# Attention slots with the products in another order, and three input projections of the second layer inside the last two slots

## The reference, cut to what matters

```python
# layer 0, for each sample b
x = normalise(x * s1)
q, k = heads(x @ Wq.T * q_dc), heads(x @ Wk.T * k_dc)
v_flat = x @ Wv.T * v_dc * s2
attn = softmax(q @ k.T * scale)                    # 16 heads of 256 x 256
out = (attn @ heads(v_flat)) @ Ww.T * w_dc + v_flat @ Wu.T * u_dc
x1 = x_in + out
# layer 1, for each sample b
xr, gate = split(x1 @ W_in.T)                      # 512 + 512 channels
xc = silu(causal_conv4(xr + t_emb) + b_conv)
xn = layernorm(xc); Bm, Cm, dt = split(xn @ W_xproj.T)
h = clip(h * ad + bd * xt, -10, 10) for each of 256 tokens; y = C h + D * xn
x2 = x1 + y * silu(gate) @ W_out.T
```

## Time and profile before

| | us |
|---|---|
| median of 3 runs | 580.69 (579.54 to 583.43) |
| the profiled execution, whole | 581.57 |
| its span in the profile | 579.8 |
| TensorE busy in the span | 481.0 (83%) |
| VectorE busy | 430.4 (74%) |
| ScalarE busy | 253.7 (44%) |
| slots 0 to 7 | about 57.8 to 265 |
| convolutions and tokens | to about 318 |
| scan over the tokens | about 368 to 579.8 |

### The profile page before, as it was taken

How to read it: one execution, slowest core, us unless ns; L and a number is a source line. 1 busy time by engine, 2 the same in 40 slices (tenths; PEclk the granted TensorE clock), 3 DMA queues, 4 the chain that set the end, 5 groups by cost and what they waited for, 6 DMA issues and landing times.

```text
span 579.8 us, 8410 instructions
## 1 busy us (share of the span) xinstructions
PE 481.0 (83%) x3000; PEld 283.4 (49%) x3000; DVE 430.4 (74%) x744; ACT 253.7 (44%) x504; POOL 194.2 (33%) x211
## 2 busy tenths in 40 slices
PE   1867888899898979879999860579999999999996
PEld 1753646567566645636999650113333333333333
DVE  2837254766756665863997995499999999999994
ACT  3331666667565645546787686024231111111111
POOL 6304303123030200000550295339876334434332
PEclk9966799999999989887999995599999999999999
DMA  8785375764846550101044447565654433443310
GB/s 343 300 154 109 56 145 112 146 118 88 152 102 137 95 115 2 37 2 36 1 175 144 133 141 184 166 222 188 200 174 91 153 107 107 124 128 111 99 31 24
DMA packets 44629, 71.80 MB, mean 124 GB/s; under 512 B 18825, under 2 KB 33545, under 8 KB 41468
## 3 DMA queue, kind: packets, MB, share of 16 engines
q1 hardware_dynamic: 40684, 67.55, 44.5%
q0 software_dynamic: 528, 3.55, 1.6%
q10 hardware_dynamic: 3376, 0.16, 0.3%
HBM read 41.88 MB, written 23.02 MB: 112 GB/s over the span
## 4 chain that ended last, share of the span: by engine, by line
PE 51%; DVE 24%; ACT 9%; DMA 6%; issue 3%; POOL 3%; SPq 2%; ACTq 0%; DVEq 0%; POOLq 0%
DVE win L1660 9%; ACT ex L682 6%; PE bank L980 6%; PE bank L1316 6%; PE bank L1276 5%; PE bank L1028 5%; PE bank L927 5%; PE bank L1287 5%; DVE z L1660 5%; PE bank L965 4%; PE bank L1007 3%; PE bank L950 3%; PE bank L998 3%; PE bank L1222 2%; DVE lnb_rep L1660 2%
## 5 line engine op out<-in xcount | busy, mean ns | idle before, releaser
L1482 DVE TENSOR_REDUCE mx<-bank 128x2 f32<-128x512 f32 x128 | 81.9, 686 | 80.2 <-PE bank L950 79.7
L1276 PE MATMUL bank<-xst,bst 128*128 128x512 bf16 x256 | 82.2, 390 | 41.2 <-DMA bst<-bd_d 24.9
L682 ACT ACTIVATE ex<-bank 128x512 f32<-128x512 f32 x128 | 69.8, 597 | 55.5 <-PE bank L965 55.3
L1660 DVE CUSTOM_DVE_ANT_0 win<-win,bank,hi 128x512 f32<-128x512 f32 x96 | 71.8, 748 | 3.4
L1276 PEld LDWEIGHTS bank<-xst,bst 128*128 128x128 bf16 x256 | 24.8, 98 | 94.8 <-DVE win L1660 31.0
L455 POOL TENSOR_TENSOR qk<-qk,part 128x512 f32<-128x512 f32 x16 | 19.7, 1233 | 138.2 <-ACT part L618 138.2
L950 PE MATMUL bank<-kst,qst 96*128 96x256 bf16 x256 | 49.8, 288 | 5.6 <-issue 3.4
L927 PE MATMUL bank<-xnT,w 128*128 128x256 f32 x192 | 50.5, 419 | 3.7 <-ACT xnT L603 3.6
L965 PE MATMUL bank<-qst,kst 97*128 97x256 bf16 x256 | 48.0, 283 | 4.0 <-ACT ex L682 1.9
L563 POOL TENSOR_TENSOR yg<-yT,gateT 128x128 f32<-128x128 f32 x60 | 29.4, 528 | 60.1 <-ACT yT L860 60.1
L980 PE MATMUL bank<-ex,vp 128*32 128x256 f32 x512 | 36.5, 405 | 12.9 <-ACT ex L682 12.9
(11 more groups left out here) (190 smaller groups left out, 917.0 us busy)
## 6 DMA issues: line engine op xcount, KB each, us to landing
qk_d<-part SPq DMA_DIRECT2D x64, 96.0 KB, 2.5
xs_d<-xpart SPq DMA_DIRECT2D x16, 384.0 KB, 4.6
xst<-xs_d SPq DMA_DIRECT2D x15, 384.0 KB
xn_d<-xc SPq DMA_DIRECT2D x16, 256.0 KB, 3.4
xtk<-xn_d SPq DMA_DIRECT2D x64, 64.0 KB
xst<-xs_d SPq DMA_DIRECT2D x15, 256.0 KB
bd_d<-zeros POOLq DMA_DIRECT2D x1, 3468.0 KB, 13.0
qst<-qk_d SPq DMA_DIRECT2D x8, 384.0 KB, 4.6
```

What stands on the lines that cost most here:

```text
L682: nc.scalar.activation(ex[:, n // 4, n % 4, :], bank[6 + n % 2][:, :], ACT.Exp, scale=SCALE)\
L1276: mm(bank[t % 4][:, :], bst[:, slot, t % RS, :], xst[slot][:, t % RS, :], start=True, stop=True)\
L1482: v.tensor_reduce(mx[:, :, STACKED[n]:STACKED[n] + 1], bank[4 + n % 2][:, :].rearrange("p (t k) -> p t k", t=HALVES), AX.X, ALU.max)\
L1660: v._custom_dve(bass.dve_ops.TENSOR_ADD_SAT, out=zst[t % ZR], in0=zst[(t - 1) % ZR], in1=bank[t % 4][:, :], s0=hi[:, t:t + 1], s1=0.0).the ...
```

## The change

In `sample(b)`, TensorE starts with `transpose_xn(b + 2)`, before `weigh(b - 1, 3)` and `turn_maxima(b)`; `v_tokens(b + 1)` moves from behind the maxima to behind heads 10 and 11; `weigh(b, 1)` moves behind heads 8 and 9, `weigh(b, 2)` behind heads 12 and 13, and `project_att` in front of heads 8 and 9. Heads 14 and 15 are done as pairs, maxima first. ScalarE's list follows: `take_xn` before `take_maxima`, `take_v` after the exponential of head 13, `take_weighed(b, 0)` after that of head 11.

In slot 6, `project_v(5)` and `project_v(6)` stand between the maxima and the scores, and `project_in(0)` is cut into halves of two channel blocks with heads between. In slot 7, `project_v(7)` and `project_in(1)` stand before the scores, and `project_in(2)` is made in two halves near the end. The first half of `project_in(3)` follows the slot, its second half follows `to_tokens(0)`. ScalarE copies the projections and does the last tap in single pieces of one channel block between exponentials (`projection_piece`, `tap_piece`). On VectorE `convolve(0)` moves from the end of slot 6 into slot 7, behind `attend(5)` and `add_skip(7)`; `attend(7)` moves behind `convolve(2)`, and `project_att(7)` behind `to_tokens(2)`. No operation is added or removed, only their order and the waits.

```diff
+            def projection_piece(b, c):
+                act.wait_ge(s["xr_done"], b * 2 + 1 + c // 2)
+                if b >= 2 and c == 0:
+                    act.wait_ge(s["conv_done"], b - 1)
+                ins = nc.scalar.activation(xrp[:, b % 2, c, TAPS - 1:],
+                                           bank[(4 if b else 2) + c // 2][:, (c % 2) * S:(c % 2 + 1) * S],
+                                           ACT.Identity, bias=cond[:, c, b:b + 1])
+                if c == CT - 1:
+                    ins.then_inc(s["xr_in"], 1)
...
             def sample(b):
                 project = b + 2 < B
-                take_maxima(b)
                 if project:
                     take_xn(b + 2, 2)
+                take_maxima(b)
                 if b >= 1:
                     take_weighed(b - 1, 1)
-                if b + 1 < B:
-                    take_v(b + 1)
                 if project:
                     take_qk(b + 2, 0, 2)
                     take_qk(b + 2, 1, 3)
+                if b == B - 2:
+                    act.wait_ge(s["ld_l1"], 16 * 11)
+                    act.wait_ge(s["const_pool"], 2)
+                elif b == B - 1:
+                    last_tap(0)
                 exponentials(b, 0, 2)
                 if project:
                     second_cast(b + 2, 0)
@@ -702,21 +716,20 @@
                 exponentials(b, 2, 4)
                 if project:
                     take_vt(b + 2, 2)
-                if b == B - 1:
-                    take_projection(1)
-                exponentials(b, 4, 10)
-                take_weighed(b, 0)
-                if b == B - 1:
-                    last_tap(1)
-                exponentials(b, 10, 12)
-                if b == B - 2:
-                    act.wait_ge(s["ld_l1"], 16 * 11)
-                    act.wait_ge(s["const_pool"], 2)
-                    take_projection(0)
-                exponentials(b, 12, 14)
-                if b == B - 2:
-                    last_tap(0)
-                exponentials(b, 14, NH)
+                for n in range(4, NH):
+                    exponentials(b, n, n + 1)
+                    if b == B - 2 and 7 <= n < 11:
+                        projection_piece(0, n - 7)
+                    elif b == B - 1 and 4 <= n < 8:
+                        projection_piece(1, n - 4)
+                    elif b == B - 1 and 8 <= n < 12:
+                        tap_piece(1, n - 8)
+                    elif b == B - 1 and 12 <= n:
+                        projection_piece(2, n - 12)
+                    if n == 11:
+                        take_weighed(b, 0)
+                    elif n == 13 and b + 1 < B:
+                        take_v(b + 1)
...
-                if b + 2 < B:
+                elif b + 2 < B:
                     take_projection(b + 2)
...
+                for half in halves:
+                    for c in (2 * half, 2 * half + 1):
+                        for k in range(HT):
+                            ins = mm(bank[(4 if b else 2) + half][:, (c % 2) * S:(c % 2 + 1) * S],
+                                     win[:, k, c * P:(c + 1) * P], xres[:, k, b * S:(b + 1) * S],
+                                     start=k == 0, stop=k == HT - 1)
+                    ins.then_inc(s["xr_done"], 1)
+            def close_maxima(b):
                 if b >= 1:
                     weigh(b - 1, 3)
                 if b == 0:
                     pe.wait_ge(s["vt_in"], 2)
-                elif b == 1:
-                    pe.wait_ge(s["k_in"], 3)
-                elif b < B - 1:
-                    pe.wait_ge(s["skip_in"], b - 1)
                 else:
-                    pe.wait_ge(s["xr_in"], 1)
+                    pe.wait_ge(s["v_in"], b + 1)
                 turn_maxima(b)
...
+            def both(b, lo, hi):
+                for n in range(lo, hi):
+                    scores(b, n, n + 1)
+                    max_scores(b + 1, n, n + 1)
             def sample(b):
...
                 if b == 0:
                     pe.wait_ge(s["k_in"], 2)
                 elif b < 3:
@@ -1055,99 +1069,88 @@
                 else:
                     pe.wait_ge(s["x1_ready"], b - 2)
                 transpose_xn(b + 2, 2)
...
+                close_maxima(b)
                 pe.wait_ge(s["xnT_ready"], b + 3)
                 channels_of(0, 2, "q_done")
...
+                pe.wait_ge(s["mT_ready"], b + 1)
                 channels_of(1, 3, "k_done")
                 scores(b, 0, 2)
                 max_scores(b + 1, 0, 2)
                 pe.wait_ge(s["q_in"], b + 3)
                 channels_of(2, 2, "vt_done")
...
+                both(b, 2, 4)
                 if b >= 1:
                     pe.wait_ge(s["k_in"], b + 3)
                     project_v(b - 1, 3)
...
+                both(b, 4, 6)
                 if b == 0:
                     pe.wait_ge(s["wgain"], 2)
                 weigh(b, 0)
...
+                both(b, 6, 8)
                 if b >= 2:
                     pe.wait_ge(s["vt_in"], b + 3)
                     project_att(b - 2, 2)
...
+                both(b, 8, 10)
+                weigh(b, 1)
+                both(b, 10, 12)
+                if b >= 1:
+                    pe.wait_ge(s["skip_in"], b)
+                else:
+                    pe.wait_ge(s["k_in"], 3)
+                v_tokens(b + 1)
+                both(b, 12, 14)
                 weigh(b, 2)
...
+                max_scores(b + 1, 14, 16)
+                scores(b, 14, 16)
...
             def last_but_one(b):
...
+                close_maxima(b)
+                pe.wait_ge(s["x1_ready"], b - 2)
+                project_v(b - 1, 2)
                 pe.wait_ge(s["mT_ready"], b + 1)
+                project_v(b, 3)
+                scores(b, 0, 2)
+                pe.wait_ge(s["skip_in"], b)
+                project_att(b - 2, 2)
+                max_scores(b + 1, 0, 2)
+                both(b, 2, 6)
+                weigh(b, 0)
+                both(b, 6, 8)
+                pe.wait_ge(s["x1_ready"], b - 1)
+                project_in(0, (0,))
+                both(b, 8, 10)
+                pe.wait_ge(s["skip_in"], b + 1)
+                project_in(0, (1,))
+                both(b, 10, 12)
+                weigh(b, 1)
+                both(b, 12, 14)
+                pe.wait_ge(s["xr_in"], 1)
                 v_tokens(b + 1)
...
+                weigh(b, 2)
+                max_scores(b + 1, 14, 16)
+                scores(b, 14, 16)
+            def last_sample(b):
+                close_maxima(b)
+                project_v(b, 2)
+                project_in(1)
                 scores(b, 0, 2)
...
                 pe.wait_ge(s["mT_ready"], b + 1)
                 project_att(b - 2, 3)
...
+                scores(b, 2, 6)
                 weigh(b, 0)
...
+                scores(b, 6, 10)
                 weigh(b, 1)
...
                 scores(b, 10, 12)
+                pe.wait_ge(s["skip_in"], b + 1)
+                project_att(b - 1, 2)
+                scores(b, 12, 14)
+                project_in(2, (0,))
                 weigh(b, 2)
...
+                scores(b, 14, NH)
+                project_in(2, (1,))
                 weigh(b, 3)
...
-            project_in(2)
+            project_in(3, (0,))
...
-                    pe.wait_ge(s["skip_in"], B)
+                    pe.wait_ge(s["x1_ready"], B - 1)
...
             for b in range(B):
                 to_tokens(b)
-                if b == 1:
-                    pe.wait_ge(s["x1_ready"], B - 1)
+                if b == 2:
                     project_att(B - 1, 3)
-                if b + 3 < B:
+                if b == 0:
+                    project_in(3, (1,))
+                elif b + 3 < B:
                     project_in(b + 3)
...
             def last_but_one(b):
                 attend(b - 2)
-                maxima(b + 1, 0, 3)
-                add_skip(b - 1, 3)
-                maxima(b + 1, 3, 5)
+                add_skip(b - 1, 2)
+                add_skip(b, 3)
+                maxima(b + 1, 0, 2)
                 add_mix(b - 2, 2)
-                maxima(b + 1, 5, NH)
+                maxima(b + 1, 2, NH)
+            def last_sample(b):
+                attend(b - 2)
+                add_skip(b, 2)
                 convolve(0)
-            def last_sample(b):
-                attend(b - 2)
-                add_skip(b - 1, 2)
                 add_mix(b - 2, 3)
-                add_skip(b, 2)
                 attend(b - 1)
-                add_mix(b - 1, 3)
+                add_mix(b - 1, 2)
                 convolve(1)
...
-            attend(B - 1)
             take_raw(0)
             for b in range(2, B):
                 convolve(b)
                 if b == 2:
+                    attend(B - 1)
+                elif b == 3:
                     add_mix(B - 1, 3)
```

More of the change, by code:

```diff
@@ L1017, in weight_sums, with project_in @@
                 ins.then_inc(s["pconst"], 1)
-            def project_in(b):
+            def project_in(b, halves=(0, 1)):
```

(42 more changed lines are left out.)

59 lines of the change are left out of this document (12 added, 47 removed).

## The result

The changed kernel takes 563.11 us (median of 4 runs, 562.12 to 564.92) against 582.06 for the kernel before on the same chip (579.54 to 584.33): ratio 0.9679, 95% interval 0.9627 to 0.9731. The profiled execution took 563.17 with a span of 561.4, 18.4 less than the one before. The prediction was 563.

What follows compares the result with a forecast made beforehand. TensorE was taken as the bound, but with holes. Gains of 7.5 (slots 0 to 5), 4.6 (slot 6) and 5.7 (slot 7 and loop), 17.8 us off the profiled 581.57, gave 563.8, stated as 563; range 556 to 571.

Steps and rivals of the forecast that it cites:

- Slots 0 to 5, in all: Slots 0 to 5: 3.2 + 0 + 6.3 - 2.0 = 7.5 us less.
- Slots 2 to 5: 22.2 us of products plus a 0.7 stall, 22.9 each; 91.6 in place of 97.9, 6.3 less.
- The stall: Slots 2 to 5: TensorE waits 0.7 us for the row of maxima in front of the scores.
- upper bound of 1.7 us: Slots 2 to 5: largest stall s if the stacks take the longest row's time, slot 23.9 us.
- Slots 0 and 1: Slot 0 gains 3.2 us without a stall; slot 1 waits some 4, gains nothing, and the clock costs 2.0.
- The row lands with the stacks: Start of each slot: the row of maxima lands 0.1 to 1 us behind the stacks, even if issued earlier.
- Slot 6: 25.3 us against 29.9, 4.6 less, with a 1.4 stall for the stacks and `max_scores` held back some 2.
- Slot 7 to the first tokens: `to_tokens(0)` 26.9 us after the turn against 34.6, 7.7 less, with ScalarE late next.
- Loop over the tokens: VectorE becomes the bound; last `take_raw` 76.3 us after slot 7's turn against 82.0, so 5.7 of 7.7 arrive.
- rival (c): Stall of 1 to 2 us delays the next stacks; slots 1 to 5 keep 24.3 us; 569.3 in all; chance 0.17.
- Rival (e): Stall over 2.1 us in each slot lowers TensorE's clock; slots 26.7 us, 589 in all; chance 0.04.

Runs made afterwards that it cites:

- changed_again: The changed kernel itself, unedited, run again later beside two other kernels: 564.90 us, ratio 0.9727 to the kernel before.
- in2_behind: Changed kernel, but `project_in(2)` made whole behind slot 7 again, with its copies in the loop over the tokens: 564.13 us, ratio 0.9713.
- attend_first: Changed kernel, but VectorE does `attend(7)` ahead of `take_raw(0)`, as before the change: 569.28 us, ratio 0.9803.
- casts_ahead: `row_uncovered`, but in slots 0 and 1 the v product precedes the scores and both second casts precede heads 0 and 1's exponentials: 559.98 us, ratio 0.9635.
- extra_dma: Changed kernel plus 384 KB moved inside DRAM, issued by SyncE behind the stack loads of samples 3 to 7: 568.37 us, ratio 0.9801.
- mix_early: Changed kernel, but VectorE does `add_mix` after maxima 7 instead of after maxima 10: 564.98 us, ratio 0.9738.
- row_uncovered: Changed kernel with `add_mix` behind maxima 7, q's second cast before heads 0 and 1's exponentials, `project_att` before slot 6's scores: 559.54 us, ratio 0.9641.

## Why the prediction was right

The time was right to 0.1 us, and that closely it was luck: run again, the changed kernel took 564.90, and its gain in the profiled execution was 18.4 us (forecast 17.8), in the medians 18.95. The sums of the stages were right to about 1 us; some of the terms in them were wrong and cancelled.

**Slots 0 to 5, in all.** Forecast 7.5 less, measured at slot 6's turn 206.12 - 198.55 = 7.6. By parts it differs. Slots 2 to 5: 91.6 forecast, 198.55 - 106.82 = 91.7 measured, 22.9 each as said. But I had put them together as 22.2 plus 0.7 for the row, and they are 22.0 plus 0.63 for VectorE's maxima plus 0.27 for the row in the mean (0.33, 0, 0.74, 0). The stall was mis-sized, since I gave every slot the mean landing; in this execution it comes only in every other slot. Its upper bound of 1.7 us was too low as well: `changed_again` waited 2.92 in slot 2. The 0.63 I had overlooked: I asked only ScalarE and the DMA what is late next, not VectorE, whose `add_mix` stands between maxima 10 and 11.

**Slots 0 and 1.** Here a step was wrong. Slot 0 was to gain 3.2 without a stall; it waits 2.60 us for its row, issued at 57.9 and landed 7.9 us later, and gains 1.4, and another 0.9 came from in front of it, since the transposes stand in the wait before the first turn. That slot 0 has no stall is wrong in the repeats of this order too (1.1 us in `in2_behind` and `attend_first`, 3.11 in `changed_again`). Slot 1 was to wait 4 and lose 2.0 by the clock; it waits 3.09 and lasts 25.45, 1.0 more than before. Without a stall it would last 20.7, from the 21.96 of `changed_again` with a wait of 1.26, so the clock cost about 1.7 by this estimate. (The row of `weigh` that the prediction calls half speed, 1.61 us against 1.07, is two thirds; the granted clock over 3 us from there is 0.56.) In sum 1.2 forecast (3.2 less the 2.0 for the clock), 1.4 measured (0.9 + 1.4 - 1.0).

**The row lands with the stacks.** Right nearly everywhere. In the changed kernel it comes 0.2 to 1.2 us behind the last stack load (as in slot 4, 157.0 and 155.9 above), whether issued 1.8 or 7.6 us before that; in slot 7, with none in flight, it takes 1.8 us. In the twelve profiles without the extra transfer 81 rows were issued while stacks were in flight, and 80 landed 0.2 to 1.5 us behind them; the other, in slot 1 of `casts_ahead`, landed 2.6 behind. In `extra_dma` traffic that nobody waits for comes between, and the row lands behind that. The rule of the Trainium skill, page "DMA: Bandwidth & Descriptors", section "Queues, rings and completion order", that an increment lands only after earlier writes of that DMA engine across queues, agrees with this; that it is this mechanism and not another that holds the row back, no run here separates.

**Slot 6.** 25.3 forecast, 25.27 measured, in part by luck: 1.55 us for the row (a stall of 1.4 forecast, but for the stacks), 1.12 for `max_scores` behind `add_mix(4)` (2 forecast), 0.96 before `weigh(3)` (1.05 forecast). Without these waits the slot is 21.6 us, where the forecast's 21.7 had the 1.05 in it and so gave the products 20.7; that and the shorter wait for `add_mix(4)` cancelled.

**Slot 7 to the first tokens.** 26.9 forecast, 26.24 measured. ScalarE is the bound, as said, with short waits of TensorE for it (0.47, 0.47, 0.46, 1.05), and the clock stays at 1.00.

**Loop over the tokens.** 5.7 of 7.7 us were to arrive, with the last `take_raw` 76.3 after the turn; 75.3 was measured. VectorE runs from `convolve(2)` at 254.32 to `convolve(7)` without a hole, as said. The stage is 1.7 us longer than before (49.1 against 47.4), and 6.7 us arrive at the last `take_raw` (75.3 against 82.0).

**Rivals.** The feedback of rival (c) did not take hold in the changed kernel: its waits in slots 2 to 5 are 0.33, 0, 0.74 and 0. Why it stayed away, no run shows. Rival (e) has its mechanism shown in slots 1 (changed kernel), 2 (`changed_again`) and 4 (`mix_early`): stall and low clock together make the last two 6 us longer than their neighbours (28.7 against 22.6, 28.0 against 21.8). In no profile did it strike two of the slots 2 to 5, and in these two the next slot has no wait for the row. So the 14 us that I worked out for all six slots were far more than any run shows.

## What to carry to other kernels

When waits on the critical engine are filled, ask of every engine and every transfer in turn what is late next: here three candidates (a DMA that lands behind bulk loads, VectorE's order, ScalarE's pace) lay close behind each other, the two remedies that I tried alone gained nothing that their runs can tell, and several together gained 0.9% or more. Run the same kernel again before a single slot is explained by an edit: here the stalls of the same order varied by more than the edits changed them. A small transfer on which the critical path depends should be in flight when nothing large is; no run here tried that, and independent work in front of its use shortened the wait but gained nothing by itself. A projection moved into a phase that ended on another engine brought nothing, though it filled TensorE's holes. What paid in the tail was that VectorE did something else while a transfer was under way (3.9 us by `attend_first`) and, as the timelines suggest but no run separates, that slots 6 and 7 kept no long hole.

## What the runs showed of the hardware

Over the thirteen profiled executions, all 17 holes of TensorE of 2.76 us or more from slot 0 into the loop over the tokens were followed by 3 us at a mean granted clock of 0.50 to 0.70; 0.50 is 1.2 GHz throughout. Of the shorter ones some were and some were not: 2.60, 2.20 and 2.18 us left it at 1.00, while 2.10 brought it to 0.56, 1.93 to 0.65 and 1.52, in the loop, to 0.75. The price beyond the hole was 1.6 us (`row_uncovered`, slot 4) to 3.2 (`mix_early`, slot 4, and `changed_again`, slot 2), each against a slot without a hole in the same execution. The 8 KB DMA of the row took between 1.8 us, with no stacks in flight, and 7.9. 384 KB from DRAM to DRAM behind 1.5 MB of loads landed only 0.6 to 0.9 us behind them, though the last of the loads took 8 to 9. The issue of a DMA on SyncE, 0.43 to 0.44 us in the median of the writes shown, took 1.57 us once among them in `mix_early` and 1.28 us once in `in2_behind`.
